# Attention products take both addends of every other unit on TensorE, rings of six, some evacuations on ScalarE

## The reference, cut to what matters

```python
h    = x @ W[cat] + b[cat]                      # conditioning
q, k, v = h @ w_qkv.T                           # 16 heads of 32
s    = q @ k.T / sqrt(32) + alibi, causal       # per head
num  = 0.5 * (1 + s * rsqrt(1 + s*s))           # rational softmax
att  = num @ v / (sum(num) + 1e-6)
x    = x + att @ w_out.T
y    = layernorm(x + relu(x @ W1 + b1) @ W2 + b2) * gamma + beta
out  = x + int8_ffn(y)                          # one scale over all of y
```

## Time and profile before

| what | value |
|---|---|
| median of 3 runs | 2264.09 us (2263.49 to 2267.63) |
| profiled execution, its own time | 2265.64 us |
| its span in the trace | 2263.8 us |
| granted TensorE clock, mean | 0.907 of full speed |

### The profile page before, as it was taken

One profiled execution on the slowest core, in us unless ns is written; L12 is line 12 of the kernel. 1 busy time (PEld: TensorE's weight loads), 2 busy tenths in 40 slices (PEclk: granted clock), 3 DMA queues, 4 the chain that ended last, 5 costly groups with the idle time before them and its releaser, 6 DMA issues.

```text
span 2263.8 us, 31228 instructions
## 1 busy us (share of the span) xinstructions
PE 1803.9 (80%) x10640; PEld 904.5 (40%) x10640; DVE 1878.6 (83%) x2114; ACT 1685.0 (74%) x1938; POOL 1715.7 (76%) x784
## 2 busy tenths in 40 slices
PE   5678877877787789998888877877787787887864
PEld 4555323333333346664444433333333333342331
DVE  4358888888889888889789898888888888899768
ACT  0247897989889888889567667999889888767413
POOL 2136887788878887788678887788878887788548
PEclk9899988988898899999999998988988898998879
DMA  5411111110111022202322221110111021121137
GB/s 176 146 49 44 49 30 35 43 45 25 40 40 49 20 69 66 68 25 74 84 77 81 69 54 34 40 49 21 45 40 48 20 79 44 42 62 52 59 123 237
DMA packets 126620, 138.68 MB, mean 61 GB/s; under 512 B 27868, under 2 KB 78044, under 8 KB 126044
## 3 DMA queue, kind: packets, MB, share of 16 engines
q1 hardware_dynamic: 126460, 136.64, 21.5%
HBM read 54.02 MB, written 22.80 MB: 34 GB/s over the span
## 4 chain that ended last, share of the span: by engine, by line
PE 38%; ACT 21%; DVE 20%; issue 12%; POOL 4%; DMA 2%; SPq 2%; DVEq 0%; POOLq 0%; ACTq 0%
ACT yb L669 9%; PE sc L825 7%; PE ov L804 7%; ACT yb L671 7%; DVE gb L1042 6%; PE dn L804 6%; ACT gb L661 6%; DVE gb L983 5%; PE it L723 5%; PE it L740 4%; PE it L747 4%; PE it L727 3%; POOL oT L654 2%; SPq L428 2%; PE it L707 1%
## 5 line engine op out<-in xcount | busy, mean ns | idle before, releaser
L623 POOL TENSOR_TENSOR yb<-yb 128x1024 f32<-128x1024 f32 (+3 forms) x640 | 1510.2, 2373 | 460.9 <-DVE gb L1042 448.6
L669 ACT ACTIVATE yb<-sc 128x1024 f32<-128x1024 f32 (+3 forms) x640 | 566.9, 886 | 376.3 <-PE sc L825 189.8
L1042 DVE TENSOR_TENSOR gb<-sc,yb 128x1024 f32<-128x1024 f32 (+3 forms) x640 | 676.6, 1057 | 186.1 <-ACT yb L671 183.9
L983 DVE TENSOR_TENSOR gb<-gb,yb 128x1024 f32<-128x1024 f32 (+3 forms) x640 | 779.2, 1218 | 3.9 <-ACT gb L661 0.5
L825 PE MATMUL sc<-qmv,kst 128*128 128x512 f32 (+3 forms) x1280 | 505.6, 472 | 295.8 <-DVE gb L1042 278.2
L671 ACT ACTIVATE yb<-yb 128x1024 f32<-128x1024 f32 (+3 forms) x640 | 595.0, 930 | 20.3
L661 ACT ACTIVATE gb<-gb 128x1024 f32<-128x1024 f32 (+3 forms) x640 | 584.1, 913 | 0.1
L825 PEld LDWEIGHTS sc<-qmv,kst 128*128 128x128 f32 x1280 | 238.7, 209 | 648.3 <-DVE gb L1042 453.3
L804 PE MATMUL ov<-gb,vv 128*32 128x512 f32 (+3 forms) x2560 | 338.4, 604 | 18.0 <-DVE den L997 10.5
L804 PE MATMUL dn<-gb,ones 128*32 128x512 f32 (+3 forms) x2560 | 326.3, 584 | 0.0
L723 PE MATMUL it<-hT,wT 128*128 128x512 f32 x496 | 249.9, 629 | 5.8 <-DVE area L921 1.8
(11 more groups left out here) (112 smaller groups left out, 1093.5 us busy)
## 6 DMA issues: line engine op xcount, KB each, us to landing
qmv<-stage SPq DMA_DIRECT2D x384, 64.0 KB
kst<-stage SPq DMA_DIRECT2D x384, 64.0 KB
area<-in_x_dram SPq DMA_DIRECT2D x58, 256.0 KB, 2.8
out_dram<-oT SPq DMA_DIRECT2D x32, 256.0 KB, 3.3
den<-rec_d SPq DMA_DIRECT2D x31, 256.0 KB
wT<-wT_d SPq DMA_DIRECT2D x7, 768.0 KB, 4.4
x_d<-area SPq DMA_DIRECT2D x16, 256.0 KB, 2.6
z_d<-area SPq DMA_DIRECT2D x16, 256.0 KB, 3.2
```

Source lines behind the costliest of these rows:

```text
L623: pool.tensor_tensor(y, y, y, ALU.mult).then_inc(s_y2, 1)
L669: act.activation(y, sc[:, k % SLOTS, :, q0_of(g, k):], ACT.Square).then_inc(s_s2, 1)
L983: dve.tensor_tensor(t, t, yview(k)[:, :, q0:], ALU.add).then_inc(s_num, 1)
L1042: dve.tensor_tensor(gview(k)[:, :, q0:], sc[:, k % SLOTS, :, q0:], yview(k)[:, :, q0:], ALU.mult).then_inc(s_g, 1)
```

## The change

Pairs get a kind by their number modulo four, `KINDS = ("split", "split", "fold", "sum")`. So units alternate.

- **split** (both pairs of every even unit): no sum on VectorE. TensorE accumulates `gb` and `yb` one after the other into `ov` and `dn`: 16 + 16 records in place of 8 + 8.
- **fold** (first pair of every odd unit): ScalarE leaves out (1 + g) squared. VectorE forms (g + 2) * g in place, and later adds 1 and y squared in a second instruction.
- **sum** (second pair of every odd unit): as before.
- The sum of a pair follows one pair behind (`SUM_LAG = 1`), not two; (1 + g) squared too (`SQUARE_LAG = 1`). The products follow two units behind (`LAG = 2`) and stand after an even pair's scores.
- Both rings have six buffers in one tensor `ring` (together twelve, as before).
- `rt`, `a` and `zt` are emptied by ScalarE, behind the activations of their pair. VectorE keeps the maximum (`largest`). GpSimd's `norm` has one more small instruction.
- The loops are gone; all eight groups are written out.

```diff
-YRING = 4
-GRING = 8
-NUM_LAG = 2
-LAG = 3
+RING = 6
+KINDS = ("split", "split", "fold", "sum")
+SQUARE_LAG = 1
+SUM_LAG = 1
+LAG = 2
...
-            if k % 2:
+            if k % 2 == 0:
...
+            def after(b, job, item, z_before):
+                what, j = job.name
+                a, m = place(b, j)
+                bank = it[:, item % BANKS] if item < REST else end_bank(item)
+                feat = bank.rearrange("p (k n) -> p k n", k=KC)
+                act.wait_ge(s_item, item + 1)
+                if what == "rt":
+                    if m:
+                        act.wait_ge(s_zst[a], 16 * m)
+                        act.wait_ge(s_amax, z_before)
+                    act.activation(resT[a], feat, ACT.Copy).then_inc(s_evac_act, 1)
+                elif what == "a":
+                    act.wait_ge(s_bw, 16 * 7 * (b + 1))
+                    act.activation(hid[a], bank[:, 0:P], ACT.Relu, bias=b1c[:, 0:1]).then_inc(s_evac_act, 1)
+                elif what == "zt":
+                    for k in range(KC):
+                        r = act.activation(resT[a][:, k, :], feat[:, k], ACT.Identity, scale=gam[:, k:k + 1],
+                                           bias=bet[:, k:k + 1])
...
+                    if n >= RING:
+                        if kind(n - RING) == "split":
+                            act.wait_ge(s_pv, (n - RING) // 2 + 1)
+                        else:
+                            act.wait_ge(s_num, summed(n - RING) + 1)
+                    act.wait_ge(s_qk, n + 1)
+                    act.activation(y, sc[:, n % SLOTS, :, q0_of(n):], ACT.Square).then_inc(s_s2, 1)
+                    act.wait_ge(s_s2, n + 1)
                     act.activation(y, y, ACT.Abs_reciprocal_sqrt, bias=1.0).then_inc(s_y, 1)
-                    if k >= NUM_LAG or g is not opening:
-                        one_plus_g_squared(G, g, k - NUM_LAG)
+                    if n >= SQUARE_LAG and kind(n - SQUARE_LAG) != "fold":
+                        one_plus_g_squared(n - SQUARE_LAG)
+                    for job in after_pair.get(k, []):
+                        d = b if g is ending else b - 1
+                        after(d, job, bases[0] + job.index, zs_before(d, job.name[1]))
...
-                pe.wait_ge(s_num, G * PAIRS + 2 * u + 2)
+                n = G * PAIRS + 2 * u
+                for m in (n, n + 1):
+                    if kind(m) == "split":
+                        pe.wait_ge(s_y2, m + 1)
+                        pe.wait_ge(s_g2, squared(m) + 1)
+                    else:
+                        pe.wait_ge(s_num, summed(m) + 1)
                 last_kb = kb == TT * (c + 1) - 1
+                heads = [(h, gview(n + h // 2)[:, h % 2, q0:], True, kind(n + h // 2) != "split") for h in range(HG)]
+                heads += [(h, yview(n + h // 2)[:, h % 2, q0:], False, True) for h in range(HG) if kind(n + h // 2) == "split"]
                 for dst, is_v in ((ov, True), (dn, False)):
-                    for h in range(HG):
+                    for h, weights, begins, ends in heads:
                         lhsT = vv[:, kb, h * D:(h + 1) * D] if is_v else ones[:, :]
-                        r = pe.matmul(dst[h * D:(h + 1) * D, q0:], lhsT, gview(2 * u + h // 2)[:, h % 2, q0:],
-                                      start=(kb == 0), stop=last_kb)
+                        r = pe.matmul(dst[h * D:(h + 1) * D, q0:], lhsT, weights,
+                                      start=(kb == 0 and begins), stop=(last_kb and ends))
...
-            def numerator(G, g, k):
-                q0 = q0_of(g, k)
-                t = gview(k)[:, :, q0:]
-                dve.wait_ge(s_y2, G * PAIRS + k + 1)
-                dve.wait_ge(s_g2, G * PAIRS + k + 1)
-                dve.tensor_tensor(t, t, yview(k)[:, :, q0:], ALU.add).then_inc(s_num, 1)
+            def fold(n):
+                g = gview(n)[:, :, q0_of(n):]
+                dve.wait_ge(s_g, n + 1)
+                dve.scalar_tensor_tensor(out=g, in0=g, scalar=2.0, in1=g, op0=ALU.add, op1=ALU.mult).then_inc(s_fold, 1)
+
+            def numerator(n):
+                g, y2 = (v[:, :, q0_of(n):] for v in (gview(n), yview(n)))
+                dve.wait_ge(s_y2, n + 1)
+                if kind(n) == "fold":
+                    dve.wait_ge(s_fold, before(n, "fold") + 1)
+                    dve.scalar_tensor_tensor(out=g, in0=g, scalar=1.0, in1=y2, op0=ALU.add, op1=ALU.add).then_inc(s_num, 1)
+                else:
+                    dve.wait_ge(s_g2, squared(n) + 1)
+                    dve.tensor_tensor(g, g, y2, ALU.add).then_inc(s_num, 1)
...
-                    if k >= GRING or carry:
-                        dve.wait_ge(s_pv, G * UNITS + (k - GRING) // 2 + 1)
-                    dve.wait_ge(s_y, G * PAIRS + k + 1)
-                    dve.tensor_tensor(gview(k)[:, :, q0:], sc[:, k % SLOTS, :, q0:], yview(k)[:, :, q0:],
+                    n = G * PAIRS + k
+                    q0 = q0_of(n)
+                    if n >= RING:
+                        dve.wait_ge(s_pv, (n - RING) // 2 + 1)
+                    dve.wait_ge(s_y, n + 1)
+                    dve.tensor_tensor(gview(n)[:, :, q0:], sc[:, n % SLOTS, :, q0:], yview(n)[:, :, q0:],
                                       ALU.mult).then_inc(s_g, 1)
-                    if k >= NUM_LAG or carry:
-                        numerator(G, g, k - NUM_LAG)
+                    if kind(n) == "fold":
+                        fold(n)
+                    if n >= SUM_LAG and kind(n - SUM_LAG) != "split":
+                        numerator(n - SUM_LAG)
```

More of the change, by code:

```diff
@@ L152, in __init__ @@
         self.operands = [job.name for job in self.items if job.name[0] in ("q", "k")]
-        assert len(self.items) % BANKS == 0 or not has_next
+        self.ranks, self.evacs = ranks(self.items)
+        assert not has_next or len(self.items) % BANKS == 0 and all(eng == "dve" for eng, _ in self.ranks[-BANKS:])
     def item(self, *name):
@@ L207, in runs @@
     def runs(b):
-        return [(0, opening if b == 0 else joining, 1), (1, plain, NG - 2), (NG - 1, ending if b == B - 1 else closing, 1)]
-    starts, n = {}, PRO
+        return ([(0, opening if b == 0 else joining)] + [(hg, plain) for hg in range(1, NG - 1)] +
+                [(NG - 1, ending if b == B - 1 else closing)])
+    starts, n = {}, (PRO, PRO, 0)
     for b in range(B):
-        for hg, g, count in runs(b):
+        for hg, g in runs(b):
             starts[b, hg] = n
-            n += count * len(g.items)
-    REST = n
+            n = tuple(v + w for v, w in zip(n, (len(g.items), g.evacs["dve"], g.evacs["act"])))
+    REST, REST_DVE, REST_ACT = n
     PRO_JOBS = woven(cond_jobs, range(TT))
     END_JOBS = woven(after_jobs, range(DONE, KB), KB - DONE)
+    END_ITEMS = [job for job in END_JOBS if job.parts]
+    END_RANKS, END_EVACS = ranks(END_ITEMS)
     PLACES = 2 + KB - DONE
@@ L411, in ops_before, with zs_before @@
             return 2 if g is opening else 2 * NC * G + 3
+        def zs_before(b, j):
+            order = [job.name[1] for job in (ending if b == B - 1 else joining).items if job.name[0] == "zt"]
+            n = KB * b
+            return n + (order.index(j - 2) + 1 if j >= 2 else 0)
         @block.sync
@@ L675, in _ @@
             act.wait_ge(s_chain, 9)
             act.wait_ge(s_wst, 48)
-            for_groups(act, group)
-            for k in range(-NUM_LAG, 0):
-                one_plus_g_squared(B * NG, plain, k)
+            for_groups(group)
+            for n in range(TOTAL - SQUARE_LAG, TOTAL):
+                if kind(n) != "fold":
+                    one_plus_g_squared(n)
+            for job, (eng, rank) in zip(END_ITEMS, END_RANKS):
+                if eng == "act":
+                    after(B - 1, job, REST + job.index, 0)
@@ L778, in project_first @@
                 for part in range(KC):
[L779 removed]
+                    r = compute(bank, Job((what, 0), []), part, 0, 0, None, 2 * TT, 0, wqT_s[:, 0])
                 r.then_inc(s_item, 1)
```

258 lines of the change are left out of this document (150 added, 108 removed).

## The result

The changed kernel takes 2527.1 us (median of 4 runs, 2524.5 to 2788.2), the kernel before beside it 2265.9 (2263.5 to 2269.0). The ratio is 1.115, interval [1.1125, 1.1171]: 261 us slower, where I forecast 2250 and drew the range up to 2325.

The account below looks back on a forecast made before the run. No engine bounds the whole kernel; the bound changes by stage: ScalarE in plain groups, TensorE in closing, VectorE in joining. Terms summed to -14 us, 2265.6 to 2251.6, median 2250 us; 8-in-10 range 2170 to 2325.

Parts of the forecast that it names:

- Handshake: A chunk's first unit, now doubled, waits for `output` at 16 places in plain groups: +14 us, between 0 and +27.
- Full-width pace: Full-width stretches: four pairs take 11.7 us in place of 11.8, some 60 cycles: -5 us, ends -57 and +13.
- rival 4: Shared SBUF pair: every sum and fold behind a GpSimd instruction, 12.0 us for four pairs, 2268 us; no separate chance.
- The clock: TensorE: denser work keeps the clock up, near 0.98 in plain groups: -25 us, between 0 and -38.
- Rival 3: TensorE's clock stays at 0.88 because its pauses at chunk starts remain: 2275 us, chance 0.10.
- Item units: Where an item meets a doubled unit, odd-pair scores come 0.5 to 1 us late: +22 us, between 0 and +72.
- rival 2: TensorE's burst decides: a doubled unit with an item in front costs 1.5 us an item; 2325 us, chance 0.26.
- Closing: Closing group: TensorE, busy 223 of 239 us, gets 31 more: +18 us, between +5 and +30.
- opening: Opening group: first three chunks, full of conditioning, get 18 us of products: +10 us, between 0 and +18.
- Joining: Joining group: VectorE falls from 283 to about 220 us, 317 becomes 297: -20 us, between -35 and +20.
- ending: Ending group: the same relief of VectorE as in joining, with 10 tiles: -10 us, between -25 and +15.
- Unrolled loops: Loop turns, where TensorE idles 2.28 us for issue: two turns go, -6 us, between 0 and -10.

Follow-up runs that it names:

- the 2255 kernel: Changed kernel with every pair summed, sums and squares two behind, products three units back behind the odd pair, output early, rings of four and eight: 2255.1 us, ratio 0.9958.
- the run at 2357.1: Changed kernel with the output back at the last product's place and kinds split, split, sum, sum, so no fold: 2357.1 us, ratio 1.0417.

## Why the prediction was wrong, by its own steps

**Handshake** (+14, bound +27). This step failed first and by most: with the output back at its place 108 us come back, 69 of them in the four plain groups that I had priced and 24 in closing. I priced the doubled unit behind the handshake, 1.72 us, and not the handshake itself, which the change had moved behind a product and a sum, ahead of which a division and evacuations may stand. The price was up to 7.6 us of TensorE's idle time at one chunk's end, products at half clock behind it, and scores queued behind those.

**Full-width pace** (-5, ends -57 and +13). Where nothing else stood in the way the cycle came to what I had worked out: pairs 36 to 39 of group 1 took 11.6 us, for 11.7. Some luck is in that: the count lets the second square end after 1.75 us, for which I had no row (the one at 597.02 took 1.89), and 60 cycles at 11.7 in place of 11.76 make -4, not -5. What failed is that the cycle stood for all of the fold and of the one-pair distance. It held ScalarE, VectorE and GpSimd, but no TensorE and no chunk's end. The fold costs 58 us where I had at most 13 lost, in good part since it stands ahead of the division, the evacuation and the copy at a chunk's end (3.0 us at each of two places in a plain group). And the price of sums one pair behind has its measure in a run: 213 us in the kernel before, where a late sum holds the next product and with it the scores. I read the earlier trace rows rightly as the situation to come, and then priced it as the sum's own delay.

The Trainium skill (SBUF — State Buffer, section SBUF: two separate sides) has a VectorE instruction with two SBUF inputs and a GpSimd instruction exclude each other. The 2.96 us beside 4.84 us of squares agree. That rule in full was my rival 4, at 2268; the fault was not in the rule but in what I let hang on it.

**The clock** (-25). It stayed at 0.89 in plain groups (0.88 before). Rival 3 says so, at a price of only 25. With the output early and no fold it is 0.94, and 0.89 in the 2255 kernel without doubled products: with most of the waits gone, denser work goes with a higher clock, as I had it.

**Item units** (+22, to +72) and rival 2. This term was too small as well: I had the scores 0.5 to 1 us late behind a doubled unit with an item, and at 600.88 ScalarE idled 2.32 us there, with TensorE away from the scores for 5.5 us (5.2 in my count). In the count over the plain groups, products and items that waited for nothing hold ScalarE 36 us longer than before, and products that waited for VectorE 148 us longer. So rival 2 had the right sign and engine and a real mechanism, but the smaller one: what mostly decides is that the burst waits, not that it is long.

**Closing** (+18, bound +30) became +54, **opening** (+10) +23. TensorE's added busy time there was 41 and 29 us. With the output early closing takes 270, opening 297.5; without the fold too, 262.4 and 287.5, which is 23 and 7 us over before. So these two terms, priced from TensorE's work alone, were near right for the work, and the handshake and the fold came on top.

**Joining** (-20) and **ending** (-10) became +24 and +25. The moved evacuations do free VectorE (252 of 307 us in the 2255 kernel, 283 before), but are worth 9.5 us in joining and -4 in ending. The two pieces above do not explain joining: with the output early it takes 345.0 us, and without the fold too 344.8. The distance does more there: in the kernel before, `NUM_LAG = 1` alone takes joining from 316.9 to 349.4, and in the changed kernel without fold, with products behind the odd pair, sums and squares two behind bring it from 344.1 to 331.6. I had let the freed VectorE time count for -20 and had not asked what sums one behind do in this group. What is left of joining was not split further.

**Unrolled loops** (-6): right, 5 us measured. **Last six tiles** (-4): the stretch behind the groups went from 121.4 to 118.0 us, right. Two of the signs of being wrong that I had named came true: joining did not shorten, and the clock stayed.

**Diagonals** (-8): not isolated in any run.

In sum: of the 261 us, 108 are the output's place and 58 the fold (170 together). The way down from 2357.1 to 2255.1 goes by +43 (odd place), -67 (sums and squares two behind), -45 (all summed, rings of four and eight) and -34 (products three back). Those four depend on each other, as the two-pair distance shows that costs 182 behind the even pair and gains 67 behind the odd one, so none of them is a price of its own. How much of the 45 is the doubled products and how much the rings stays open: three units back with split pairs, which hold their ring places longer, wasn't tried. Why the odd place costs 43 us while sums stand one behind was measured, not traced to one wait.

## What to carry to other kernels

Before pricing added work on an engine with in-order instructions, write down for each of its waits what stands ahead of the releaser on the other engine, and what queues behind the waiter: a distance of one pair less cost 213 us here with not one instruction added. Software-pipeline distances and places in the order are one setting, not several: the same `2` was worth -67 or +182 us (in the first case the squares moved with the sums). And go through the diff for statements that only change place; the one that I left out cost 108 us, where the largest term that I priced was 25.

## What the runs showed that I had not expected

- GpSimd's next square gets ahead of a VectorE sum that waits only for the square just ended. Above, the second of two squares runs until 598.91, the sum issued at 597.03 until 599.99, 1.1 us later. Over all 640 sums the mean is 1487 ns one pair behind (the kernel before with `NUM_LAG = 1`) and 1229 two behind (the 2255 kernel).
- The division of a chunk (128x512, both inputs in SBUF) took 2082 ns on average in the changed kernel and 888 in the run at 2357.1, for the same 31 instructions. In the places looked at the difference is whether it starts ahead of GpSimd's square (0.68 us) or behind it (2.38). A single VectorE instruction put in front of it, here the fold, decides that.
- Emptier engines did not make a faster kernel: in the run at 2357.1 a plain group has VectorE at 158 us and GpSimd at 151 (198 and 191 before), a clock of 0.94 in place of 0.88, and takes 239.8 us in place of 232.5.
